# A gated cross-attention stack on one core: the distance bias made by GpSimd, two weights loaded to other homes, and a new order for the ternary passage

## What is computed

```python
x = x + tanh(g_xattn[0]) * attention_0(layernorm(x), ctx)            # 16 heads of 16
x = x + tanh(g_ffn[0])   * ternary_ffn(layernorm(x))                 # 256 -> 1024 -> gelu -> 256
x = x + tanh(g_xattn[1]) * attention_1(layernorm(x), ctx, distances) # scores - log(dist + 1e-9) * |scale|
x = x + tanh(g_ffn[1])   * expert_ffn(x)                             # relu, then its own layer norm
```

## Time and profile before

| what | value |
|---|---|
| the profiled execution's own time | 393.59 us |
| its span | 391.9 us |
| ScalarE (ACT) busy | 282.4 us, 72% |
| VectorE (DVE) busy | 285.9 us, 73% |
| TensorE (PE) busy | 326.0 us, 83% |
| GpSimd (POOL) busy | 231.3 us, 59% |
| mean granted TensorE clock | 0.955 |
| slots 4 to 7 of layer 1 | 60.2 to 108.3 us |
| ternary passage, first rounding to first queries of layer 2 | 129.06 to 192.66 us |

### The profile page before, as it was taken

The page is one execution under the profiler, slowest core; times in us unless marked ns, Lnnn a source line. Parts: engine busy times, 40 slices in busy tenths (PEclk is TensorE's granted clock), DMA queues, the critical chain, the costliest instruction groups (busy, mean ns, idle before and its releaser), DMA issues.

```text
span 391.9 us, 8930 instructions
## 1 busy us (share of the span) xinstructions
PE 326.0 (83%) x3222; PEld 266.3 (68%) x3222; DVE 285.9 (73%) x684; ACT 282.4 (72%) x516; POOL 231.3 (59%) x405
## 2 busy tenths in 40 slices
PE   2868988678886786897777999999798899999992
PEld 2547767566763653565555888778687799888882
DVE  5987688875899999669366555887756558666667
ACT  4565899899886899989634789767669767555540
POOL 2585766767796225658727557556874276554442
PEclk9995899999899899979899999999999999999997
DMA  8796555100100004000451222222000000000001
GB/s 221 172 163 127 151 158 139 43 22 23 44 25 0 2 24 57 2 0 0 143 139 40 54 55 53 52 54 53 5 2 2 2 2 28 28 29 27 28 28 54
DMA packets 23187, 22.02 MB, mean 56 GB/s; under 512 B 4711, under 2 KB 22504, under 8 KB 23067
## 3 DMA queue, kind: packets, MB, share of 16 engines
q1 hardware_dynamic: 23144, 21.45, 22.5%
HBM read 10.34 MB, written 2.10 MB: 32 GB/s over the span
## 4 chain that ended last, share of the span: by engine, by line
PE 43%; ACT 21%; DVE 16%; issue 11%; DMA 3%; POOL 3%; SPq 1%; ACTq 0%; POOLq 0%; DVEq 0%
PE psA L1889 10%; PE psBE L1873 5%; PE psA L1688 4%; PE psD L1873 4%; PE psD L1597 3%; DMA xs<-in_x 3%; ACT pp_hi L775 3%; ACT wspace L846 3%; DVE mx L1239 2%; ACT p L766 2%; PE psA L1672 2%; PE psBE L1623 2%; PE psA L1846 2%; ACT space L831 2%; ACT xn L739 1%
## 5 line engine op out<-in xcount | busy, mean ns | idle before, releaser
L497 POOL TENSOR_TENSOR pp_lo<-p,pp_hi 124x512 f16<-124x512 f32 x80 | 96.9, 1232 | 39.5 <-ACT pp_hi L775 39.4
L406 POOL TENSOR_TENSOR lns<-lns,mhalf 128x2 f32<-128x2 f32 x39 | 28.5, 732 | 75.4 <-DVE lns L1007 74.9
L1239 DVE TENSOR_REDUCE mx<-psBE 128x6 f32<-128x462 f32 (+1 forms) x96 | 54.6, 581 | 25.2 <-PE psBE L1623 24.8
L766 ACT ACTIVATE p<-psD 124x512 f32<-124x512 f32 x80 | 47.6, 595 | 28.6 <-PE psD L1597 28.1
L1597 PE MATMUL psD<-qb,ktb 98*124 98x256 f16 (+1 forms) x256 | 48.8, 290 | 6.6 <-DMA qb<-mT 5.7
L775 ACT ACTIVATE pp_hi<-p 124x512 f16<-124x512 f32 x80 | 50.4, 629 | 0.2
L1597 PEld LDWEIGHTS psD<-qb,ktb 98*124 98x124 f16 (+1 forms) x256 | 32.7, 144 | 11.4 <-DMA qb<-mT 7.6
L1623 PE MATMUL psBE<-kt_hi,q_hi 128*128 128x154 f16 (+2 forms) x160 | 34.0, 281 | 3.0 <-ACT mT L757 2.2
L1323 DVE TENSOR_TENSOR pp_lo<-space,pp_hi 128x512 f16<-128x512 f32 x32 | 25.6, 822 | 13.3 <-ACT space L868 13.2
L1889 PE MATMUL psA<-ew_lo,pp_hi 128*128 128x256 f16 x128 | 34.9, 273 | 0.0
L1889 PE MATMUL psA<-ew_hi,pp_lo 128*128 128x256 f16 x128 | 34.9, 273 | 0.0
(11 more groups left out here) (210 smaller groups left out, 990.8 us busy)
## 6 DMA issues: line engine op xcount, KB each, us to landing
qb<-q_hi SPq DMA_DIRECT2D x32, 128.0 KB
xs<-in_x SPq DMA_DIRECT2D x8, 256.0 KB, 5.6
qb<-q_lo SPq DMA_DIRECT2D x16, 128.0 KB
tw_raw<-in_tw SPq DMA_DIRECT2D x2, 1024.0 KB, 5.6
space<-in_ew SPq DMA_DIRECT2D x2, 1024.0 KB, 6.6
out<-space SPq DMA_DIRECT2D x7, 256.0 KB, 2.1
ktb<-km SPq DMA_DIRECT2D x6, 248.0 KB, 5.8
qb<-bT_lo SPq DMA_DIRECT2D x8, 104.0 KB
```

Source lines behind the costliest of these rows:

```text
L406: nc.gpsimd.tensor_tensor(lns[:, n % 4, 1, :], lns[:, n % 4, 0, :], mhalf[:, :], ALU.pow).then_inc(s_rs, 1)
L497: nc.gpsimd.tensor_tensor(pl[:, u % 2, 2 * r:2 * r + 2, :], p32[:, n % 4, :, :], ph[:, u % 2, 2 * r:2 * r + 2, :], ALU.subtract).then_inc( ...
L766: a_(p32[:, n % 4, :, :], psD[n % 2][0:KR, :].rearrange("p (t r) -> p t r", t=2), ACT.Exp, scale=1.0 / SSC).then_inc(a["exp"], 1)
L1239: v.tensor_reduce(pairs[:, MP[k][0]:MP[k][1]:MP[k][2], :], psBE[:, n % 2, 0:hn * KEYS].rearrange("p (q e k) -> p q e k", e=2, k=KEYS), AX. ...
```

## The change

The list of each engine is touched. In words:

- `wraw[1, "o"]` and `wraw[1, "q"]` get the places of the first layer's key and value weights; SyncE waits for `s_wkp` and `s_vp` before these two loads.
- ScalarE no longer makes `bN` and `bT[0]`; GpSimd does, with `bias_natural` at the start of slots 6 and 7 and `bias_high` between the last `plo`. `bias_high` and `bias_low` read `distT2`, a copy of the transposed distances that SyncE makes by a DMA in slot 7, into the place of the first ternary weight. The gelu of unit 0 waits for `s_bn` and `d_dT2` in place of `s_bias`.
- `weights_hi(1, "q")` moves from slot 4 to behind `high(0, 6, 2)`, `weights_hi(1, "o")` from slot 5 to behind the first queries of layer 2, `split_low` from before the passage to behind slot 1 of layer 2.
- The orders of the ternary passage change on ScalarE, VectorE, TensorE and GpSimd. On GpSimd `plo(0, 7, 4)` comes before the factors of unit 4.

```diff
+        wraw[1, "o"], wraw[1, "q"] = wraw[0, "k"], wraw[0, "v"]
+        distT2 = tw_raw[0:KEYS, 0, :]
...
             shift_rows(0, 3)
+            sp.wait_ge(s_wkp, 1)
+            sp.wait_ge(s_vp, 1)
             load_w(1, "qo")
             for u in range(4, NU):
                 query_blocks(0, u)
+                if u == NU - 1:
+                    sp.wait_ge(s_ln, 2)
+                    sp.wait_ge(s_tw, 4)
+                    sp.dma_start(distT2, distT[:, :]).then_inc(d_dT2, 16)
                 shift_rows(0, u)
...
+            def bias_natural(i):
+                t = slice(i * NT // 2, (i + 1) * NT // 2)
+                pool.wait_ge(s_ln, 2)
+                pool.wait_ge(s_gsc, 3)
+                nc.gpsimd.tensor_tensor(bN[:, t, :], distN[:, t, :],
+                                        dcol[:, 0:1].unsqueeze(2).to_broadcast([128, NT // 2, KEYS]), ALU.mult).then_inc(s_bn, 1)
+            def bias_high(i):
+                c = slice(i * N // 2, (i + 1) * N // 2)
+                pool.wait_ge(d_dT2, 16)
+                nc.gpsimd.tensor_tensor(bT[0][:, c], distT2[:, c], dcol[0:KEYS, 0:1].to_broadcast([KEYS, N // 2]),
+                                        ALU.mult).then_inc(s_bt, 1)
...
+                if s in (6, 7):
+                    bias_natural(s - 6)
                 attn_slot(0, s)
...
             plo(0, 6, 3)
+            bias_high(0)
             plo(0, 6, 4)
             plo(0, 7, 0)
             plo(0, 7, 1)
+            bias_high(1)
             plo(0, 7, 2)
             plo(0, 7, 3)
+            plo(0, 7, 4)
             factors_act(NU + 4, 1.0, A[0]["fac"])
-            plo(0, 7, 4)
...
             ternary_factors(2)
+            ternary_factors(3)
+            ternary_factors(4)
             ternary_normalised(2)
+            ternary_normalised(3)
             ternary_biased(2)
-            ternary_factors(3)
-            ternary_normalised(3)
             ternary_biased(3)
-            ternary_factors(4)
             ternary_normalised(4)
             ternary_biased(4)
...
# ScalarE, setup and the lists
-                if s == 5 and r in (1, 4):
-                    act.wait_ge(s_ln, 2)
-                    act.wait_ge(s_gsc, 3)
-                    a_(bN[:, t, :], distN[:, t, :], ACT.Copy, scale=dcol[:, 0:1])
-                if s == 6 and r in (1, 4):
-                    a_(bT[0][:, c], distT[:, c], ACT.Copy, scale=dcol[0:KEYS, 0:1]).then_inc(s_bt, 1)
-                if s in (4, 5) and r == 3:
-                    weights_hi(1, "qo"[s - 4])
...
             high(0, 6, 2)
+            weights_hi(1, "q")
             exponent(0, 6, 3)
...
             outputs_hi(0, 5)
-            normalised(0, 4)
             ternary_rounded(0, 0)
             ternary_rounded(0, 1)
-            rounded(4)
             ternary_hidden(1, 0)
             ternary_hidden(1, 1)
             outputs_hi(0, 6)
             ternary_transposed(0, 0)
+            ternary_transposed(0, 1)
+            normalised(0, 4)
...
             ternary_transposed(6, 0)
-            ternary_out(2)
+            ternary_out(0)
             ternary_transposed(6, 1)
+            ternary_out(1)
             ternary_rounded(7, 0)
             ternary_rounded(7, 1)
-            ternary_out(3)
+            ternary_out(2)
             ternary_transposed(7, 0)
             ternary_transposed(7, 1)
+            ternary_out(3)
             ternary_out(4)
             queries_hi(1, 0)
+            weights_hi(1, "o")
...
# VectorE
-                if l == 0 and s == 7:
-                    bias_low(0)
...
-            bias_low(1)
             ternary_round(1, 0)
             divide(0, 5)
-            split_low(1, wraw[1, "o"], whl[1, "o"])
             ternary_round(1, 1)
             ternary_round(1, 2)
+            bias_low(0)
             ternary_round(1, 3)
-            residual_stats(0, 4, NU)
-            split_keys(1)
-            keys_high(1, 0)
+            bias_low(1)
             divide(0, 6)
             ternary_max(0, 0)
             ternary_max(0, 1)
             ternary_inverse(0)
...
             keys_high(1, 3)
+            split_low(1, wraw[1, "o"], whl[1, "o"])
             attn_slot(1, 2, 3 * NU)
...
# TensorE, the end of the passage
             ternary_transposed(5, 1)
             ternary_product(4)
-            ternary_hidden(7, 0)
-            ternary_hidden(7, 1)
-            pe.wait_ge(F["xTh"], 2)
             tables_vo(1, 3)
+            ternary_transposed(6, 0)
             ternary_product(5)
-            ternary_transposed(6, 0)
             ternary_transposed(6, 1)
             pe.wait_ge(s_vo, 16)
+            ternary_out_transposed(0)
+            ternary_out_transposed(1)
+            ternary_product(6)
             ternary_out_transposed(2)
-            ternary_out_transposed(3)
-            ternary_product(6)
             ternary_transposed(7, 0)
             ternary_transposed(7, 1)
+            ternary_out_transposed(3)
             ternary_out_transposed(4)
```

More of the change, by code:

```diff
@@ L1434, in _ @@
             ternary_inverse(3)
+            quantise(0, 6)
+            ternary_scale(3)
+            ternary_stats(1)
+            split_keys(1)
+            keys_high(1, 0)
+            keys_high(1, 1)
             quantise(0, 7)
-            ternary_scale(3)
-            ternary_residual(2)
             ternary_max(4, 0)
@@ L1782, in attn_slot @@
                             pe.wait_ge(d_w[0, "o"], 16)
+                        if s == 3 and l == 1:
+                            pe.wait_ge(s_spl, 1)
                         project(l, s - 3)
```

130 lines of the change are left out of this document (62 added, 68 removed).

## The result

The changed kernel is slower by about 1%: 397.50 us median of 4 runs (396.99 to 398.81) against 393.80 of the kernel before on the same chip, ratio 1.0099, 95% interval 1.0063 to 1.0134. In a second measurement (run e5) it was 1.0069, interval 1.0043 to 1.0094. The forecast was 391.8 with a range from 389.4 to 395.5: the time lies outside it, and the sign was wrong. The profiled execution took 396.99 us, its span is 395.2 and its mean granted clock 0.950 (0.955 before).

What follows compares the result with a forecast made beforehand. The prediction took ScalarE to bound the slots and the ternary passage, VectorE the stretch between. From 393.6 us, -2.7 (slots) + 0.2 (behind slot 7) + 0.7 (passage) = -1.8 gave 391.8 us, range 389.4 to 395.5.

Steps and rivals of the forecast that it cites:

- Slots, -2.7: Slots 4 to 7: ScalarE, relieved of weight copies and biases, saves 0.7 us in slot 5 and 2.0 in slot 6.
- SyncE: Slot 0 waits and the distT2 copy in slot 7: the added waits and any delayed row copies cost 0.
- Behind slot 7, +0.2: Slot 7 to first ternary_max: VectorE sheds 3.3 us, but bias_low waits for GpSimd's bias_high until 123.7; net +0.2 us.
- Rival B: Behind slot 7: GpSimd and VectorE take turns under a lock, 2 us later; total 393.6, no change; chance 0.17.
- The passage, +0.7: Ternary passage: -0.3 us without stalls, ending with GpSimd's 8.8 us chain, plus 1.0 for stalls; +0.7 us.
- D: Passage's last 15 us: TensorE at its low clock, +5.4 us over before; total 396.5, slower; chance 0.12.
- Layer 2, 0: Layer 2: moved weight copy and split_low fall into waits, key_blocks(1) is needed only in slot 1; cost 0.
- C: Slots: GpSimd's factors and plo set slot 6, only 0.7 us won; total 393.8, no change; chance 0.17.

Runs made afterwards that it cites:

- e5: The changed kernel itself, unedited, measured again for more executions: 396.61 us, ratio 1.0069 to the kernel before.
- e2: The changed kernel, but ScalarE makes both biases in slots 5 and 6 again and GpSimd neither: 394.19 us, ratio 0.9984 to the kernel before.
- e4: The changed kernel with GpSimd's bias_high shrunk to 16 columns in each half, the rest left 0: 394.30 us, ratio 0.9990 to the kernel before.
- e7: The changed kernel with 37 unused matmuls filling TensorE's idle time before layer 2's first queries: 395.65 us, ratio 1.0048 to the kernel before.
- e3: The changed kernel with GpSimd's ternary_biased(2) and (3) moved behind ternary_normalised(4): 396.41 us, ratio 1.0048 to the kernel before.
- e8: e6 plus e3's edit, with ScalarE making the transposed bias's high half behind the gelus of unit 0: 393.02 us, ratio 0.9966 to the kernel before.
- e6: The changed kernel with VectorE's first ternary_max ahead of both bias_low and the last rounding: 395.88 us, ratio 1.0033 to the kernel before.
- e9: e8 with the last rounding before the maximum, bias_low and bias_high(1) later, query-weight copy back in slot 4: 388.96 us, ratio 0.9894 to the kernel before.

## Why the prediction was wrong, point by point

**Slots, -2.7: right in size, partly by luck.** Measured -2.56: slot 4 -0.02, slot 5 -0.81, slot 6 -1.39, slot 7 -0.34 (forecast 0, -0.7, -2.0, 0). The clock was 1.00 in slots 4 to 6 of both profiles, so the relief itself is the 2.2 us of slots 5 and 6; slot 6 gave less than I had put. The 0.34 of slot 7 is luck with the clock: before, it ran at 0.85. In the thirteen profiles that have it at 1.00 it takes 11.08 to 11.10 us, in e2 too, which has the biases on ScalarE. `bN` took 1.21 and 1.22 us in GpSimd's idle time, cost 0, as forecast. **SyncE**, 0: right.

**Behind slot 7, +0.2: wrong, +2.1, and this is the step that failed.** I let bias_high delay `bias_low` through GpSimd's list, up to 123.7 us, and wrote that "the two engines slow each other", sharing the loss in part. In fact GpSimd was early: bias_high(1) was done at 117.44 us, which is 120.3 when the slots are counted as before (they ended 2.84 us earlier), 3.4 ahead of the forecast, since `plo` and bias ran at full length. VectorE lost instead, 9.5 us over what its operations take alone (15.71 against 6.2), and `bias_low` was late because VectorE was: bias_low(1) started at 123.31, 5.9 us after its bias_high. Rival B had the lock and also the size, +2.0 on the stretch (the 0.2 of the sum and its 1.8), but not the way: it let the two engines take turns fairly, with GpSimd ending at 125.8. The rows show unfair turns. My evidence against B, that seven `plo` and 7 us of VectorE's work fitted into 11.58 us, came from a case without bias_high. Shown by e2 and e4: without GpSimd's bias among the `plo` the stretch is 4.8 and, with its length alone taken away, 3.3 us shorter.

**The passage, +0.7: the mechanism right in the main, the size too small.** To the first queries, where the forecast ended it, it took 64.9 us (128.31 to 193.20) instead of 63.6, +1.3. ScalarE's work grew by 1.1 us (60.70 to 61.82; forecast 1.0, the normalised row of unit 4). Its waits were 3.1 us, 0.8 more than the 2.3 before. GpSimd's chain at the end was 8.9 us from 183.39 to 192.25, forecast 8.8, but it began 55.1 us behind the first rounding and not 53.8; the 1.0 us that I had put on top for stalls covers most of that. The chain that ended last begins with VectorE's statistics: GpSimd's list has the factors of unit 4 ahead of the normalised rows of unit 2, and they started only at 181.52. But the first output transposition, which I had named, was done at 183.14, 0.25 us before the chain began. Both were late, so moving the factors alone would have won little. **D** did not happen: in the last 15 us before the queries the clock was 0.96 (before 0.89), and the last three products took 1.91, 1.91 and 1.92 us. A low clock came behind the passage.

**Layer 2, 0: wrong, +2.15 in the profiled execution, none of it new work.** `wo_hi` (0.63 us at 197.03) lies in a wait of ScalarE, and `split_low` (0.68 at 218.40) lies behind both stretches. What the rows show is a low clock: 3.06 us of queries in place of 1.97, and slot 1 at 0.87. Why it was low there stays open: at the queries the idle time ahead doesn't decide it (e5 and e7 above), and slot 1 at 0.87 is a draw: before, e3, e4, e7 and e8 show 1.00, the ten other profiles 0.87. What the clock costs in the mean can't be told from one profile of each kernel. The executions of before have a mean clock of 0.9547, the 7 of the changed kernel 0.9503; by the slope above, an estimate, that is 0.7 us of the 2.7 that e5 shows.

**C** did not happen: the slots didn't wait for GpSimd. The range ended at 395.5, since I gave D only half its place and never put B's stretch, a longer passage and a loss of clock together, which is what came.

## What to carry to other kernels

Work moved from a full engine to an idle one must be priced on the third engine that shares something with the idle one: here 4 us of GpSimd's work cost VectorE 4.8, on the path. Put GpSimd's large operations where neither two-input operations of VectorE nor its large tensor_scalar (3.29 in place of 0.47 us) are due, and look at single durations of VectorE beside them, not at the sum of both. When a wait goes away (the gelus no longer needed the bias), move what it had held in order, or the engine behind just waits longer: ScalarE idled 6.99 us there. e6 made that stretch 5.6 us shorter, and e8 (0.9966) and e9 (0.9894), which also placed the rest, are faster than the kernel before.

## What was not expected of the hardware

- A VectorE operation of 0.75 us stayed out over a bias_high and two `plo`, 4.49 us (six profiles alike), and a tensor_scalar of 0.47, with one large input, 3.28. The `plo` that held it out were as long as alone (1.15), while `ternary_max`, a reduction, took 1.2 us for each half in every profile.
- The granted clock of TensorE fell in different stages in different executions: the same slot 1 took 11.60 us at 1.00 or 13.25 at 0.87, and slots 4 to 7 had their one low stretch in slot 5, in slot 6, in slot 7 or not at all. So a stage is compared slot by slot, at like clock. The executions of one kernel spread over 389.7 to 396.7 us: the intervals here, from 6 to 12 executions, are 0.5 to 0.9% wide, so a difference of well under 1% needs at least as many.
